# The bias of the damage units as three bf16 rows in TensorE's strain product, and gelus without a bias pointer

## The chip, the core and the metric

The kernel runs on one core of a Trainium2 chip. Its metric is the device time of one execution in microseconds, as the median of several runs. A core has a matrix engine (TensorE, PE in the rows), a vector engine (VectorE, DVE), an activation engine (ScalarE, ACT), a general engine (GpSimd, POOL) and a queue engine for transfers (SyncE, SP). They run side by side and wait for each other through semaphores. Each executes its own instructions in order.

## What is computed

Two layers act on x of 4 x 512 x 128. Each adds an attention and a mixture of experts. The change touches the first layer's attention alone, for 16 heads with 16 units each, a window of 64 steps:

```python
disp_win = _windows(disp, delta)
strain = disp_win - disp[:, :, :, None, :]
bond_act = gelu(strain @ W_strain + rel_emb @ W_pos)
bond_logits = (bond_act @ W_bond)[..., 0]
damage_act = gelu(strain @ W_dmg + b_dmg)
damage = sigmoid((damage_act @ W_dmg_out)[..., 0] + b_dmg_out[0])
logits = bond_logits - 10.0 * damage
```

The product with W_dmg is linear, so the kernel multiplies first and takes the difference of the windows afterwards: the damage units at offset j need gelu(AD[t + j] - AD[t + 63] + b_dmg). b_dmg has 16 values, one for each unit, and the same ones for each head.

## The kernel before

**Setup** (0 to 41 us). x is normalised, turned and multiplied into `AD` (128 partitions = 8 heads x 16 units; index 0 holds the bond units, 1 the damage units; 4 batches of 576 columns, of which 512 are time steps). ScalarE's queue issues small loads at its start, the last nine of them on `d_attn_w`; ScalarE, VectorE and TensorE each wait for all nine. VectorE builds `eyes` near the end of its list (L359 to L361: an identity and a negative identity of 32 x 32, bf16, in three blocks of partitions), then adds the residual (L365), takes the gates' scores from TensorE (L367) and makes the routing (L140 to L169). Within this it waits once for an exp of ScalarE (L429), which stands in ScalarE's list behind the copies of `AD` and two of the turned weights.

**The bank phases** (41 to 327.6 us and 406 to 693 us), one for each of two groups of eight heads. Each has 64 items, one for each offset j, in eight rounds of eight. An item has a bond half and a damage half, each of 128 partitions x 4 batches x (T - t0) columns; t0 is 60 at the first items and falls to 0. VectorE's `strain` (L580) makes the bond half in a ring of four slots; in most items of n not in `PE_ITEMS` (1, 2, 4, 6, 7) it makes the damage half as well, with `bdmg` as its scalar. For items in `PE_ITEMS` TensorE makes the damage half into two PSUM banks (`SD`), half an item at a time (L747): the fp32 values of AD are split into three bf16 parts that stand one below the other in `DS` (partitions 0 to 31, 32 to 63, 64 to 95), and a product with the identity over 96 partitions adds the parts up again. Eight matmuls bring in column t + j with the identity, eight subtract column t + 63 with the negative one. ScalarE takes the gelu of such a half from PSUM and adds the bias through a pointer (L672 and L677, `bias=bdmg[:, 0:1]`), and between them the gelu of the bond half (L675). For the other items one gelu takes both halves from the ring (L667). TensorE reduces every item to logits (L725), and its count `items_reduced` frees the slot for VectorE. Between the items VectorE, ScalarE and TensorE work on the experts: `hidden` (L754) needs w1s, a copy made by POOL (L567), `glu_in` (L600) takes its result, `expert_out` (L760) and `combine` (L612) end it.

**The head of a phase.** ScalarE and VectorE make the three parts; SP carries them to `DS` (L554, 12 transfers, `d_parts`) once POOL has cleared the pads of DS (L558, L559; `ds_zero`). POOL then copies w1s (`stage(0)`), and fills parts of Z. VectorE makes the items 0 to 2, waits for `d_parts` and takes the first hidden product (`glu_in(0)`). TensorE starts with `hidden(0)`, and waits for `d_parts` before its first strain.

**The tail.** After the last item of VectorE what is left runs in a chain through ScalarE's gelus of the items 5 to 7, TensorE's strains and reductions, the last expert's output, the tanh (L682) and VectorE's L595.

Of the kernel before, what the change touches and what calls it, by code (L numbers as in the profile page):

```python
# [11 lines left out]
F32 = mybir.dt.float32  # L12
# [8 lines left out]
P = 128  # L21
# [73 lines left out]
def dram_rows(tensor, offset, dims):  # L95
    return bass.AP(tensor=tensor.tensor, offset=tensor.offset + offset, ap=dims)
# [75 lines left out]
def first_layer(nc, t_in, l0, sb, psum, sem, ident, ACC, nhalf, stats, mv, rstd, carried):  # L172
# [14 lines left out]
    bdo = sb("bdo", [P, 1], F32, l0)  # L187
    wval = sb("wval", [P, C], F32, l0)
    lones = sb("lones", [P, 4, 32], F32, l0)
    eyes = sb("eyes", [P, 2, 32], BF16, l0)  # L190
    AD = sb("AD", [P, 2, B, TP], F32, l0)
    Z = sb("Z", [P, JQ, T], F32, l0)

# [9 lines left out]
    with ExitStack() as su:  # L203
# [16 lines left out]
        gscT = sb("gscT", [P, T], F32, su)  # L220
        gb = sb("gb", [P, E0], F32, su)
        scl = sb("scl", [P, 1], F32, su)
        mask8 = sb("mask8", [P, HG], F32, su)
        ones8 = sb("ones8", [P, HG], F32, su)
        mt = sb("mt", [WIN, WIN], F32, su)
# [86 lines left out]
        def _(v):  # L312
# [30 lines left out]
            scaled(0, 1, TF, tf_ready)  # L343
            scaled(1, 1, TF, tf_ready)
            scaled(3, 0, XN, xn_ready)
            v.wait_ge(d_attn_w, 16 * 9)
            v.wait_ge(const_ready, 2)
            for s in range(2):
                v.tensor_tensor(wblk[:, s, :, :], wrep[:, s, :].unsqueeze(1).to_broadcast([P, HG, BD]),
# [7 lines left out]
                for a in range(4):  # L357
                    last = v.tensor_scalar(lred[:, s, a, a:32:4], mask8[:], wcol[:, s:s + 1], None, ALU.mult)
            for n in range(3):  # L359
                v.tensor_copy(eyes[32 * n:32 * n + 32, 0, :], ident[32 * n:32 * n + 32, 32 * n:32 * n + 32])  # L360
                v.tensor_scalar(eyes[32 * n:32 * n + 32, 1, :], ident[32 * n:32 * n + 32, 32 * n:32 * n + 32], -1.0, None, ALU.mult)  # L361
            v.tensor_scalar(bdo[:], bdo[:], 0.5, None, ALU.mult)

            v.wait_ge(xn_ready, B)
# [8 lines left out]
        def _(act):  # L373
            wd = t_in["L0_attn_W_disp"]
            with nc.allow_non_contiguous_dma(reason="small weights"):
                act.dma_start(gw[:], t_in["L0_ffn_gate_w"]).then_inc(d_gate_w, 16)
                act.dma_start(rel[:], t_in["L0_attn_rel_pos_emb"]).then_inc(d_gate_w, 16)
                act.dma_start(b1r[:], t_in["L0_ffn_mlp1_b"]).then_inc(d_gate_w, 16)
                act.dma_start(wdisp[:], wd.rearrange("k (g n) -> k g n", g=G)).then_inc(d_gate_w, 16)
                for s, n in enumerate(("L0_attn_W_strain", "L0_attn_W_dmg")):  # L380
                    act.dma_start(wrep[:, s, :], dram_rows(t_in[n], 0, [[0, HG], [BD, BD], [1, BD]])).then_inc(d_attn_w, 16)
                act.dma_start(wpos[:], dram_rows(t_in["L0_attn_W_pos"], 0, [[BD, BD], [0, HG], [1, BD]])).then_inc(d_attn_w, 16)
                act.dma_start(scl[:], dram_rows(t_in["L0_ffn_scale"], 0, [[1, P], [1, 1]])).then_inc(d_attn_w, 16)
                for s, n in enumerate(("L0_attn_W_bond", "L0_attn_W_dmg_out")):
                    act.dma_start(wcol[:, s:s + 1], dram_rows(t_in[n], 0, [[0, HG], [1, BD], [1, 1]])).then_inc(d_attn_w, 16)
                act.dma_start(gb[:], dram_rows(t_in["L0_ffn_gate_b"], 0, [[0, P], [1, E0]])).then_inc(d_attn_w, 16)
                act.dma_start(bdmg[:], dram_rows(t_in["L0_attn_b_dmg"], 0, [[0, HG], [1, BD], [1, 1]])).then_inc(d_attn_w, 16)
                act.dma_start(bdo[:], dram_rows(t_in["L0_attn_b_dmg_out"], 0, [[0, P], [1, 1]])).then_inc(d_attn_w, 16)

            def turned_rows(b):  # L390
# [15 lines left out]
            turned_rows(0)  # L406
            turned_rows(1)
            turned_rows(2)
            act.wait_ge(d_attn_w, 16 * 9)
            turned_gates(0)  # L410
            turned_gates(1)
            turned_weights(0)
# [24 lines left out]
        def _(pe):  # L437
# [36 lines left out]
            weights(0)  # L474
            weights(1)
            pe.wait_ge(misc_sb, 1)
            pe.wait_ge(d_attn_w, 16 * 9)
            pe.matmul(S[0][:, 256:256 + WIN], wpos[:].rearrange("k h c -> k (h c)"), relT[:], start=True, stop=True).then_inc(misc_pe, 1)
            rows(3)
            pe.wait_ge(blk_ready, 2)  # L480
# [48 lines left out]
    for g in range(G):  # L529
        with ExitStack() as lp:  # L530
# [16 lines left out]

            @block.sync
            def _(sp):
                sp.wait_ge(ds_zero, g + 1)  # L550
                for n, ready in enumerate((part1, part2, part3)):
                    sp.wait_ge(ready, g + 1)
                    for q in range(4):
# [3 lines left out]
            def _(pool):  # L557
                pool.memset(DS[0:96, :, :, 0:PAD], 0.0)  # L558
                pool.memset(DS[0:96, :, :, PAD + T:TP], 0.0).then_inc(ds_zero, 1)  # L559
                if g == 0:  # L560

                    pool.sem_inc(items_reduced, RING)  # L562
# [97 lines left out]
            def _(act):  # L660
                def gelu(n, it, between=None):
# [7 lines left out]
                    f = 2 * pe_item(g, it, n)  # L669
                    tiles = ring[:, slot, 0, :, t0:T]  # L670
                    act.wait_ge(sd_ready, f + 1)
                    act.activation(ring[:, slot, 1, 0:2, t0:T], SD[:, :, t0:T], ACT.Gelu, bias=bdmg[:, 0:1]).then_inc(sd_taken, 1)  # L672
                    if between:
                        between()
                    act.activation(tiles, tiles, ACT.Gelu)  # L675
                    act.wait_ge(sd_ready, f + 2)
                    act.activation(ring[:, slot, 1, 2:4, t0:T], SD[:, :, t0:T], ACT.Gelu, bias=bdmg[:, 0:1]).then_inc(gelu_done, 1)  # L677

                def tanh(par, q):
                    act.wait_ge(items_reduced, RING + N0 + 4 * q + 4)  # L680
# [36 lines left out]
            def _(pe):  # L717
# [11 lines left out]
                def strain(n, it, half):  # L729
# [10 lines left out]
                    elif it:  # L740
                        pe.wait_ge(gelu_done, N0 + 8 * it - 8 + PE_ITEMS[-1] + 1)
                    if n == FIRST_PE_ITEMS[0] and it == 0 and half == 0:
                        pe.wait_ge(d_parts, 192 * (g + 1))
                    for sign, at in ((0, j + t0), (1, PAD + t0)):
                        for i in range(2):
                            for q in range(4):
                                mm = pe.matmul(SD[32 * q:32 * q + 32, i, t0:T], eyes[0:96, sign, :], DS[0:96, q, 2 * half + i, at:at + T - t0],  # L747
                                               start=(sign == 0), stop=(sign == 1))
                    mm.then_inc(sd_ready, 1)

                def hidden(c, u, staged):
# [1344 lines left out]
```

## Time and profile before

| | us |
|---|---|
| median of three runs | 1254.11 |
| lowest and highest run | 1249.81, 1258.18 |
| span of the profiled execution | 1203.6 |
| TensorE busy | 1056.1 (88%) |
| VectorE busy | 962.4 (80%) |
| ScalarE busy | 821.7 (68%) |
| POOL busy | 168.1 (14%) |

The span goes from the first to the last instruction of one execution; the time of a run also holds what lies around it. Busy time of TensorE is modelled, since its matmuls are pipelined. The shares are means over phases of different kinds, so the phases are to be read one by one.

### The profile page before, as it was taken

How to read it: one execution, taken by the hardware profiler on the slowest of the kernel's cores; microseconds unless marked ns; L12 is line 12 of the kernel's file. 1: busy time of each engine (PE TensorE's matmuls, PEld its weight loads, DVE VectorE, ACT ScalarE, POOL GpSimd, SP SyncE). 2: the span in 40 equal slices, each digit the busy share in tenths (PEclk: the TensorE clock that was granted, in tenths of full speed). 3: DMA queues.
4: the chain of work that ended last, by engine and by line, in shares of the span. 5: the costliest groups of instructions: out<-in, count | busy, mean ns of one | idle time of the engine just before them, and what ended most of it. 6: DMA issues, size and time to landing. Idle time of an engine off the chain costs nothing. (4 is left out here: it accounts for less than half of the span.)

```text
span 1203.6 us, 23755 instructions
## 1 busy us (share of the span) xinstructions
PE 1056.1 (88%) x9995; PEld 567.0 (47%) x9995; DVE 962.4 (80%) x1193; ACT 821.7 (68%) x888; POOL 168.1 (14%) x265
## 2 busy tenths in 40 slices
PE   6499888998879499889899868999999999999897
PEld 4233333333368333333333368853654565655533
DVE  7899999999763799999999863557778577676757
ACT  3689999999763489999989862243156666665464
POOL 5100000000140100000000050232760000000072
PEclk9699999999979789999999979999779999999899
DMA  8400000000075200000000057000132344523121
GB/s 269 128 2 2 1 1 2 1 1 2 1 204 145 54 1 2 1 1 2 1 1 2 1 172 178 24 1 1 36 105 62 105 132 125 155 80 90 47 60 45
DMA packets 71754, 67.45 MB, mean 56 GB/s; under 512 B 6148, under 2 KB 63200, under 8 KB 71648
## 3 DMA queue, kind: packets, MB, share of 16 engines
q1 hardware_dynamic: 66264, 55.31, 16.1%
q0 software_dynamic: 3840, 10.43, 3.3%
q8 instruction: 79, 1.29, 0.4%
q10 hardware_dynamic: 1544, 0.20, 0.1%
q14 instruction: 27, 0.22, 0.1%
HBM read 41.80 MB, written 20.97 MB: 52 GB/s over the span
## 5 line engine op out<-in xcount | busy, mean ns | idle before, releaser
L580 DVE SCALAR_TENSOR_TENSOR ring<-AD,PT 128x1808 f32<-128x1808 f32 (+15 forms) x128 | 286.1, 2235 | 3.8 <-POOLq L562 1.9
L725 PE MATMUL LG<-ring,lred 128*32 128x456 f32 (+15 forms) x2048 | 233.4, 575 | 2.0 <-ACT ring L677 2.0
L1932 DVE TENSOR_REDUCE MX<-SS 128x2 f32<-128x1024 f32 x119 | 144.6, 1219 | 55.3 <-PE SS L1649 55.2
L1862 ACT ACTIVATE EX<-SS 128x1024 f32<-128x1024 f32 x128 | 130.4, 1031 | 80.4 <-PE SS L1649 79.8
L667 ACT ACTIVATE ring<-ring 128x3616 f32<-128x3616 f32 (+15 forms) x50 | 169.9, 3398 | 3.7 <-DVE ring L580 3.7
L747 PE MATMUL SD<-DS,eyes 96*32 96x456 bf16 (+15 forms) x2496 | 156.2, 369 | 10.1 <-ACT ring L672 8.1
L675 ACT ACTIVATE ring<-ring 128x1824 f32<-128x1824 f32 (+15 forms) x78 | 141.0, 1808 | 0.0
L747 PEld LDWEIGHTS SD<-DS,eyes 96*32 96x32 bf16 x2496 | 58.0, 96 | 154.6 <-ACT ring L672 56.7
L580 DVE SCALAR_TENSOR_TENSOR ring<-AD,bdmg 128x1808 f32<-128x1808 f32 (+15 forms) x50 | 111.4, 2228 | 0.0
L725 PEld LDWEIGHTS LG<-ring,lred 128*32 128x32 f32 x2048 | 59.4, 110 | 100.2 <-issue 76.6
L760 PE MATMUL PY<-w2T,xg 128*128 128x128 f32 x512 | 75.6, 292 | 31.5 <-DVE xg L605 31.5
L754 PE MATMUL PH<-tT,w1s 128*128 128x512 f32 x128 | 74.5, 666 | 30.2 <-DVE xg L600 23.2
L672 ACT ACTIVATE ring<-SD,bdmg 128x912 f32<-128x912 f32 (+15 forms) x78 | 82.8, 1062 | 23.6 <-PE SD L747 21.7
L760 PEld LDWEIGHTS PY<-w2T,xg 128*128 128x128 f32 x512 | 63.2, 194 | 66.0 <-DVE xg L605 51.5
L677 ACT ACTIVATE ring<-SD,bdmg 128x912 f32<-128x912 f32 (+15 forms) x78 | 82.6, 1059 | 2.4 <-PE SD L747 1.5
L612 DVE SCALAR_TENSOR_TENSOR ACC<-PY,route,ACC 128x128 f32<-128x128 f32 x256 | 72.7, 359 | 9.2 <-PE PY L760 9.2
L567 POOL COPY w1s<-w1T 128x128 f32<-128x128 f32 x16 | 11.6, 724 | 463.9 <-PE PH L754 463.9
L1649 PE MATMUL SS<-KS,QS 32*128 32x512 f32 x238 | 62.1, 515 | 14.2 <-DVE MX L1932 12.3
L1839 ACT ACTIVATE HB<-PHh,b1c 128x128 f32<-128x128 f32 x156 | 44.6, 371 | 38.1 <-PE PHh L1601 37.8
L1669 PE MATMUL PW<-EX,VA 128*32 128x512 f32 x512 | 68.5, 609 | 0.0
L1649 PE MATMUL SS<-QS,KS 32*128 32x512 f32 x256 | 65.1, 509 | 3.2 <-ACT EX L1862 2.1
L1984 DVE RECIPROCAL attT<-attT 128x128 f32<-128x128 f32 (+1 forms) x58 | 54.5, 959 | 0.2
(346 smaller groups left out, 1558.0 us busy)
## 6 DMA issues: line engine op xcount, KB each, us to landing
w1s<-in_L_ffn_W SPq DMA_DIRECT2D x39, 256.0 KB, 3.0
w2s<-in_L_ffn_W SPq DMA_DIRECT2D x39, 256.0 KB, 2.9
band<-zs SPq DMA_DIRECT2D x8, 1024.0 KB, 9.9
wide<-band POOLq DMA_DIRECT2D x16, 380.0 KB, 8.3
wide<-band SPq DMA_DIRECT2D x16, 380.0 KB, 10.0
band<-Z SPq DMA_DIRECT2D x4, 1024.0 KB, 7.7
xs<-Z SPq DMA_DIRECT2D x4, 640.0 KB, 8.0
xl<-xs SPq DMA_DIRECT2D x10, 256.0 KB, 2.9
```

What stands on the lines that cost most here:

```text
L580: return v.scalar_tensor_tensor(out=ring[:, slot, s, :, t0:T], in0=AD[:, s, :, j + t0:j + T], scalar=extra, in1=AD[:, s, :, PAD + t0:PAD + T],
L667: act.activation(tiles, tiles, ACT.Gelu).then_inc(gelu_done, 1)
L672: act.activation(ring[:, slot, 1, 0:2, t0:T], SD[:, :, t0:T], ACT.Gelu, bias=bdmg[:, 0:1]).then_inc(sd_taken, 1)
L675: act.activation(tiles, tiles, ACT.Gelu)
L677: act.activation(ring[:, slot, 1, 2:4, t0:T], SD[:, :, t0:T], ACT.Gelu, bias=bdmg[:, 0:1]).then_inc(gelu_done, 1)
L725: mm = pe.matmul(LG[32 * b:32 * b + 32, par, s, t0:T], lred[:, s, n % 4, :], ring[:, slot, s, b, t0:T], start=(n % 4 == 0), stop=(n % 4 == 3))
L747: mm = pe.matmul(SD[32 * q:32 * q + 32, i, t0:T], eyes[0:96, sign, :], DS[0:96, q, 2 * half + i, at:at + T - t0], start=(sign == 0), stop= ...
L754: pe.matmul(PH[:], w1s[:], tT[:, c, :], start=True, stop=True).then_inc(h_ready, 1)
L760: mm = pe.matmul(PY[:, i, :], xg[:, c % 2, P * i:P * i + P], w2T[:, bass.ds(HG * g + it, 1), :].rearrange("p o c -> p (o c)"), start=True, ...
L1649: mm = pe.matmul(bank[:, n, :], rows[r:r + 32, b % 2, q, P * t:P * t + P], cols[r:r + 32, b % 2, q, :], start=True, stop=True)
L1862: act.activation(EX[:, Q % 2, hh:hh + 2, t, :], SS[:, slot, :, :], ACT.Exp, scale=SCALE1).then_inc(freed[slot], 1)
L1932: v.tensor_reduce(MX[:, t, p // 2, hh:hh + 2], pairs_of(b, name), AX.X, ALU.max).then_inc(freed[slot], 1)
```

## The change

The bias of the damage units goes into the product of the strain. `eyes` has five blocks: four positive ones and a negative one. DS gets three more partitions (96 to 98) that hold 1.0 everywhere, and block q of `eyes` has in these three rows the bf16 parts of the 32 biases of its output rows. The first eight matmuls of a half item now take 99 partitions and block q, the other eight take 96 and the negative block as before. The gelus of L672 and L677 lose their bias argument. The bias is loaded a second time as a row on three partitions (one more transfer in ScalarE's queue, so that three engines wait for ten), and VectorE splits it in seven small operations, each waiting for the one before. POOL sets the ones after the pads and waits for this before it copies w1s; TensorE waits for it before the first strain.

```diff
@@ -187,7 +187,7 @@
     bdo = sb("bdo", [P, 1], F32, l0)
     wval = sb("wval", [P, C], F32, l0)
     lones = sb("lones", [P, 4, 32], F32, l0)
-    eyes = sb("eyes", [P, 2, 32], BF16, l0)
+    eyes = sb("eyes", [P, 5, 32], BF16, l0)
     AD = sb("AD", [P, 2, B, TP], F32, l0)
     Z = sb("Z", [P, JQ, T], F32, l0)
 
@@ -220,6 +220,8 @@
         gscT = sb("gscT", [P, T], F32, su)
         gb = sb("gb", [P, E0], F32, su)
         scl = sb("scl", [P, 1], F32, su)
+        brow = sb("brow", [P, 2, P], F32, su)
+        bpart = sb("bpart", [P, 4, P], BF16, su)
         mask8 = sb("mask8", [P, HG], F32, su)
         ones8 = sb("ones8", [P, HG], F32, su)
         mt = sb("mt", [WIN, WIN], F32, su)
@@ -343,7 +345,7 @@
             scaled(0, 1, TF, tf_ready)
             scaled(1, 1, TF, tf_ready)
             scaled(3, 0, XN, xn_ready)
-            v.wait_ge(d_attn_w, 16 * 9)
+            v.wait_ge(d_attn_w, 16 * 10)
             v.wait_ge(const_ready, 2)
             for s in range(2):
                 v.tensor_tensor(wblk[:, s, :, :], wrep[:, s, :].unsqueeze(1).to_broadcast([P, HG, BD]),
@@ -357,8 +359,19 @@
                 for a in range(4):
                     last = v.tensor_scalar(lred[:, s, a, a:32:4], mask8[:], wcol[:, s:s + 1], None, ALU.mult)
             for n in range(3):
-                v.tensor_copy(eyes[32 * n:32 * n + 32, 0, :], ident[32 * n:32 * n + 32, 32 * n:32 * n + 32])
-                v.tensor_scalar(eyes[32 * n:32 * n + 32, 1, :], ident[32 * n:32 * n + 32, 32 * n:32 * n + 32], -1.0, None, ALU.mult)
+                v.tensor_copy(eyes[32 * n:32 * n + 32, 0:4, :],
+                              ident[32 * n:32 * n + 32, 32 * n:32 * n + 32].unsqueeze(1).to_broadcast([32, 4, 32]))
+                v.tensor_scalar(eyes[32 * n:32 * n + 32, 4, :], ident[32 * n:32 * n + 32, 32 * n:32 * n + 32], -1.0, None, ALU.mult)
+            r = slice(96, 99)
+            link(v.tensor_copy(bpart[r, 0, :], brow[r, 0, :]))
+            link(v.tensor_tensor(brow[r, 1, :], brow[r, 0, :], bpart[r, 0, :], ALU.subtract))
+            link(v.tensor_copy(bpart[r, 1, :], brow[r, 1, :]))
+            link(v.tensor_tensor(brow[r, 0, :], brow[r, 1, :], bpart[r, 1, :], ALU.subtract))
+            link(v.tensor_scalar(bpart[r, 3, :], bpart[r, 0, :], ident[r, 96:97], 1.0, ALU.mult, ALU.mult))
+            link(v.scalar_tensor_tensor(out=bpart[r, 2, :], in0=bpart[r, 1, :], scalar=ident[r, 97:98], in1=bpart[r, 3, :],
+                                        op0=ALU.mult, op1=ALU.add))
+            v.scalar_tensor_tensor(out=eyes[r, 0:4, :].rearrange("p q m -> p (q m)"), in0=brow[r, 0, :], scalar=ident[r, 98:99],
+                                   in1=bpart[r, 2, :], op0=ALU.mult, op1=ALU.add)
             v.tensor_scalar(bdo[:], bdo[:], 0.5, None, ALU.mult)
 
             v.wait_ge(xn_ready, B)
@@ -385,6 +398,7 @@
                     act.dma_start(wcol[:, s:s + 1], dram_rows(t_in[n], 0, [[0, HG], [1, BD], [1, 1]])).then_inc(d_attn_w, 16)
                 act.dma_start(gb[:], dram_rows(t_in["L0_ffn_gate_b"], 0, [[0, P], [1, E0]])).then_inc(d_attn_w, 16)
                 act.dma_start(bdmg[:], dram_rows(t_in["L0_attn_b_dmg"], 0, [[0, HG], [1, BD], [1, 1]])).then_inc(d_attn_w, 16)
+                act.dma_start(brow[96:99, 0, :], dram_rows(t_in["L0_attn_b_dmg"], 0, [[0, 3], [0, HG], [1, BD]])).then_inc(d_attn_w, 16)
                 act.dma_start(bdo[:], dram_rows(t_in["L0_attn_b_dmg_out"], 0, [[0, P], [1, 1]])).then_inc(d_attn_w, 16)
 
             def turned_rows(b):
@@ -406,7 +420,7 @@
             turned_rows(0)
             turned_rows(1)
             turned_rows(2)
-            act.wait_ge(d_attn_w, 16 * 9)
+            act.wait_ge(d_attn_w, 16 * 10)
             turned_gates(0)
             turned_gates(1)
             turned_weights(0)
@@ -474,7 +488,7 @@
             weights(0)
             weights(1)
             pe.wait_ge(misc_sb, 1)
-            pe.wait_ge(d_attn_w, 16 * 9)
+            pe.wait_ge(d_attn_w, 16 * 10)
             pe.matmul(S[0][:, 256:256 + WIN], wpos[:].rearrange("k h c -> k (h c)"), relT[:], start=True, stop=True).then_inc(misc_pe, 1)
             rows(3)
             pe.wait_ge(blk_ready, 2)
@@ -547,7 +561,7 @@
 
             @block.sync
             def _(sp):
-                sp.wait_ge(ds_zero, g + 1)
+                sp.wait_ge(ds_zero, 2 * g + 1)
                 for n, ready in enumerate((part1, part2, part3)):
                     sp.wait_ge(ready, g + 1)
                     for q in range(4):
@@ -557,6 +571,8 @@
             def _(pool):
                 pool.memset(DS[0:96, :, :, 0:PAD], 0.0)
                 pool.memset(DS[0:96, :, :, PAD + T:TP], 0.0).then_inc(ds_zero, 1)
+                pool.memset(DS[96:99], 1.0).then_inc(ds_zero, 1)
+                pool.wait_ge(ds_zero, 2 * g + 2)
                 if g == 0:
 
                     pool.sem_inc(items_reduced, RING)
@@ -669,12 +685,12 @@
                     f = 2 * pe_item(g, it, n)
                     tiles = ring[:, slot, 0, :, t0:T]
                     act.wait_ge(sd_ready, f + 1)
-                    act.activation(ring[:, slot, 1, 0:2, t0:T], SD[:, :, t0:T], ACT.Gelu, bias=bdmg[:, 0:1]).then_inc(sd_taken, 1)
+                    act.activation(ring[:, slot, 1, 0:2, t0:T], SD[:, :, t0:T], ACT.Gelu).then_inc(sd_taken, 1)
                     if between:
                         between()
                     act.activation(tiles, tiles, ACT.Gelu)
                     act.wait_ge(sd_ready, f + 2)
-                    act.activation(ring[:, slot, 1, 2:4, t0:T], SD[:, :, t0:T], ACT.Gelu, bias=bdmg[:, 0:1]).then_inc(gelu_done, 1)
+                    act.activation(ring[:, slot, 1, 2:4, t0:T], SD[:, :, t0:T], ACT.Gelu).then_inc(gelu_done, 1)
 
                 def tanh(par, q):
                     act.wait_ge(items_reduced, RING + N0 + 4 * q + 4)
@@ -740,12 +756,16 @@
                     elif it:
                         pe.wait_ge(gelu_done, N0 + 8 * it - 8 + PE_ITEMS[-1] + 1)
                     if n == FIRST_PE_ITEMS[0] and it == 0 and half == 0:
+                        pe.wait_ge(ds_zero, 2 * g + 2)
                         pe.wait_ge(d_parts, 192 * (g + 1))
-                    for sign, at in ((0, j + t0), (1, PAD + t0)):
-                        for i in range(2):
-                            for q in range(4):
-                                mm = pe.matmul(SD[32 * q:32 * q + 32, i, t0:T], eyes[0:96, sign, :], DS[0:96, q, 2 * half + i, at:at + T - t0],
-                                               start=(sign == 0), stop=(sign == 1))
+                    for i in range(2):
+                        for q in range(4):
+                            pe.matmul(SD[32 * q:32 * q + 32, i, t0:T], eyes[0:99, q, :], DS[0:99, q, 2 * half + i, j + t0:j + T],
+                                      start=True, stop=False)
+                    for i in range(2):
+                        for q in range(4):
+                            mm = pe.matmul(SD[32 * q:32 * q + 32, i, t0:T], eyes[0:96, 4, :], DS[0:96, q, 2 * half + i, PAD + t0:PAD + T],
+                                           start=False, stop=True)
                     mm.then_inc(sd_ready, 1)
 
                 def hidden(c, u, staged):
```

## Rows read from the trace of the kernel before

**Rows 1.** Busy times by stretch, us: stretch, length, PE, PEld, DVE, ACT, POOL, clock, DMA.

```profile
100.00:300.00 200.00, 182.88 (x1936) 72.75 (x1928) 200.00 (x217) 188.10 (x144) 4.09 (x6) 0.99 0.01 1
300.00:327.60 27.60, 23.08 (x228) 9.29 (x228) 21.50 (x31) 22.21 (x17) 0.00 (x0) 1.00 0.00 1
```

**Rows 2.** What VectorE waited for, 41 to 327.6 us: total us, times, longest.

```profile
DVE ACC L612 <- PE PY L760: 4.6, 3, 2.9
DVE Z L595 <- ACT Z L682: 2.6, 2, 1.5
DVE ring L580 <- PE LG L725: 0.8, 1, 0.8
DVE xg L600 <- DMA DS<-xg: 0.4, 1, 0.4
```

**Rows 3.** The page's costliest groups: busy us, mean ns, idle before: the bank gelus.

```profile
L672 ACT ACTIVATE ring<-SD,bdmg 128x912 f32<-128x912 f32 (+15 forms) x78 | 82.8, 1062 | 23.6 <-PE SD L747 21.7
L677 ACT ACTIVATE ring<-SD,bdmg 128x912 f32<-128x912 f32 (+15 forms) x78 | 82.6, 1059 | 2.4 <-PE SD L747 1.5
```

**Rows 4.** Groups of one shape (60 to 320 us), and the page's exp from PSUM.

```profile
L672 ACT ACTIVATE ring<-SD,bdmg 128x1024 f32<-128x1024 f32 x3 | 3.3, 1108 | 0.1
L1862 ACT ACTIVATE EX<-SS 128x1024 f32<-128x1024 f32 x128 | 130.4, 1031 | 80.4 <-PE SS L1649 79.8
```

**Rows 5.** Instructions in order of time, tail of the first phase: start us, us.

```profile
313.94 1.09 ACT L672 ACTIVATE ring<-SD,bdmg 128x1024 f32<-128x1024 f32 x1
...
319.05 1.11 ACT L672 ACTIVATE ring<-SD,bdmg 128x1024 f32<-128x1024 f32 x1
...
320.22 1.05 PE L747 MATMUL SD<-DS,eyes 96*32 96x512 bf16 x16 [0.19 <-ACT ring L672]
...
321.09 1.89 PE L725 MATMUL LG<-ring,lred 128*32 128x512 f32 x16
...
324.11 1.13 DVE L612 SCALAR_TENSOR_TENSOR ACC<-PY,route,ACC 128x128 f32<-128x128 f32 x4 [2.92 <-PE PY L760]
```

**Rows 6.** POOL's memset of 4096 elements by shape; the copy of w1s, min/median/max ns.

```profile
L1476 POOL MEMSET VA<- 128x4096 f32 x1 | 3.5, 3511 | 3.9 <-POOLq L1107 3.9
L567 POOL COPY w1s<-w1T x16: 289/729/1474, 42.0 to 645.0; 128x128 f32<-128x128 f32 x16
```

**Rows 7.** Instructions in order of time, head of the first phase.

```profile
41.10 0.94 POOL L558 MEMSET DS<- 96x1008 bf16 x1 [16.47 <-POOLq L203]
...
41.16 2.10 DVE L580 SCALAR_TENSOR_TENSOR ring<-AD,PT 128x1808 f32<-128x1808 f32 x1 [1.88 <-POOLq L562]
...
42.03 1.39 POOL L567 COPY w1s<-w1T 128x128 f32<-128x128 f32 x1
...
43.47 2.07 PE L754 MATMUL PH<-tT,w1s 128*128 128x512 f32 x2 [3.05 <-POOL w1s L567]
...
49.74 2.10 DVE L580 SCALAR_TENSOR_TENSOR ring<-AD,PT 128x1808 f32<-128x1808 f32 x1
...
56.27 0.75 DVE L600 TENSOR_SCALAR xg<-PH,b1T 128x512 f32<-128x512 f32 x1 [0.41 <-DMA DS<-xg]
```

**Rows 8.** Instructions in order of time, setup.

```profile
8.22 0.61 ACTq L387 DMA_DIRECT2D bdmg<-in_L_attn_b_dmg  x1
...
8.87 2.31 ACTq L388 DMA_DIRECT2D bdo<-in_L_attn_b_dmg_out  x1
...
18.64 1.26 ACT L402 ACTIVATE tT<-su,scl 128x512 f32<-128x512 f32 x2 [1.72 <-DMA bdo<-in_L_attn_b_dmg_out]
...
28.38 0.42 DVE L367 TENSOR_TENSOR gsc<-su,gb 128x256 f32<-128x256 f32 x1 [1.17 <-PE su L499]
...
32.99 0.29 DVE L156 TENSOR_TENSOR c<-c 128x128 f32<-128x128 f32 x1
...
37.21 0.41 ACT L429 ACTIVATE route<-route 128x256 f32<-128x256 f32 x1
...
37.65 0.42 DVE L166 TENSOR_TENSOR route<-route,gt 128x256 f32<-128x256 f32 x1 [2.33 <-ACT route L429]
```

## The prediction

> **What bounds the kernel now.** The span of the profiled execution is 1203.6 us, the median of the runs 1254.11 us, so 50.5 us lie around the span; I take them as fixed and make the sum against the median. The change works in two bank phases (41 to 327.6 us, and again from 406 us), so I read the busy times of each engine by stretch first. From 100 to 300 us VectorE is busy for 200.00 of 200 us, ScalarE for 188.1, TensorE for 182.9 [rows 1]; the second phase reads the same. The reader is to see that ScalarE has 11.9 us and TensorE 17.1 us free there, and VectorE none. The end of the phase is different: from 300 to 327.6 us VectorE is busy for 21.50 and ScalarE for 22.21 of 27.6 us, so there other engines set the pace.
>
> Next the waits of VectorE over the whole phase: 4.6 us for TensorE's PY in 3 waits, 2.6 us for ScalarE's tanh in 2, 0.8 us for the first reduction, 0.4 us for the DMA of the strain parts [rows 2]. That is 8.4 us of 286, and none of it lies between 100 and 300 us. What ScalarE or TensorE save in between frees nothing: VectorE's item (L580) is what the next gelu waits for.
>
> **The gelus without a pointer.** 156 bank gelus (L672 and L677, 78 each) take 82.8 and 82.6 us together [rows 3]. Each has its input in PSUM and its bias in `bdmg`. At 1024 columns one takes 1108 ns; the nearest activation without a pointer, the exp of the second layer, also from PSUM and of 1024 columns, has a mean of 1031 ns [rows 4]. I take 77 ns a gelu. The other end is nothing (were the new form to read a constant by pointer all the same). 156 x 0.077 = 12.0 us of ScalarE's busy time, 6.0 us a phase. The Trainium skill, ScalarE: Activation LUTs (What ACT_TABLE_LOAD costs), states about 93 ns for each pointer operand; by that it would be 14.5 us. Either way it is busy time of an engine that is not the bound.
>
> How much of it reaches the end? At the tail I follow the order in time [rows 5]. The chain runs through L672 of item 6, its other tiles, L677 of item 6, then TensorE's strain for item 7, L672 of item 7 at 319.05, TensorE's second strain at 320.22, reduction at 321.09, an expert's product, and VectorE's L612 at 324.11 after a wait of 2.92 us. Three bank gelus lie in this chain (L672 and L677 of item 6, L672 of item 7); L677 of item 7 runs beside the reduction. So the tail shrinks by 3 x 0.077 = 0.23 us. At the head, VectorE's one wait for PY stands behind the strain that waits for one L672: 0.08 us. With 0.31 us a phase, both give 0.6 us. The lower bound is 0. The upper one is all of the 8.0 us that other engines cost VectorE [rows 2], which needs a gain ten times that of the gelus in the chains, so it is no end of the range.
>
> **TensorE's strain with 99 rows.** The number of matmuls stays: 16 for each half item, the same columns, the same accumulation; only the first eight take 99 rows for 96 and another slice of `eyes`. 16 of them with 512 columns take 1.05 us, 16 passes of the fp32 reduction with 128 rows and 512 columns 1.89 us [rows 5]. Those are the ends: nothing, and the price of the row with 128 rows (another type, hence far off). I take nothing, since three rows in 96 even at a cost in proportion to rows would be 0.03 us a group, 78 groups a phase, 2.6 us, which lies in TensorE's free time: 17.1 of 200 us [rows 1], about 22 us over the 260 us of the phase with strains, or 0.29 us a group. Without that cover it would be 5 us in all.
>
> **The row of ones by POOL.** The memset of DS[96:99] is 4 x 4 x 576 = 9216 bf16 elements in each partition. The memset of 1008 such elements took 0.94 us [rows 7], one of 4096 fp32 elements 3.51 us [rows 6]: 0.83 ns an element. So 0.94 + 8208 x 0.00083 = 7.8 us. It stands ahead of the copy of w1s (L567), ended until now at 43.4 us, and of the fill of Z, which nobody waits for. POOL is free for the copy at 42.0 + 7.8 = 49.8 us. The copy takes 1.39 us there and ends with VectorE's item that began before it [rows 7]; over all copies it takes 289 to 1474 ns [rows 6]. The item beginning at 49.74 ends at 51.8, so I put the copy's end at 52.0. The first expert product (2.07 us there) then ends at 54.1. VectorE takes it at 56.27, and waited there for a DMA, not for the product [rows 7]. Margin 2.1 us: cost nothing. SP's DMAs wait for the pads' memset alone (the count stays the first of the two), so d_parts comes as before; TensorE's new wait for the ones stands before its first strain, and that comes later than the 56.27 us of L600. If the cover were gone, each us of POOL beyond a 9.9 us memset would delay VectorE by one, twice.
> The Trainium skill, SBUF — State Buffer (Who interferes with whom), says that the port pair which VectorE and GpSimd share is an exclusive lock for whoever comes first, and excepts GpSimd instructions that only write; without that exception the memset would hold VectorE's items, at the price of the rival below. The rows bear the exception out: the item at 41.16 took 2.10 us beside the memset of 0.94, and the one at 49.74, with POOL idle, 2.10 as well [rows 7].
>
> **The setup.** ScalarE's queue issues one DMA more, ahead of `bdo`'s. The nearest issues took 0.61 us (`bdmg`) and 2.31 us (`bdo`, which came into a backlog) [rows 8]; I take 0.6. ScalarE itself, VectorE and TensorE wait for the last of these at 18.64 us, 7.5 us after its issue, when the large weights are in; so it comes 0 to 2.3 us later, I take 0.6. Behind ScalarE's wait stand the turned gates, behind VectorE's the block weights, the lower tiles and its new work. That work: three copies wider by 96 columns, 0.1 us each, and seven operations of 128 columns on three partitions, each waiting for the one before. One of 128 columns took 0.29 us [rows 8]; 0.32 with the wait, so 2.2 us; 2.5 us in all. VectorE had idle time behind it: 1.17 us before L367, and 2.33 us at L166 while ScalarE came late to its exp (0.41 us of it is the exp): 1.9 us of slack [rows 8]. 0.6 + 2.5 = 3.1 us against 1.17 + 1.9 = 3.1 us. So it just fits: I take 0.1 us; the upper end is 2.3 + 2.5 - 3.1 = 1.7 us. What is late next, once the slack is gone, is ScalarE's exp, behind it two turned weights, TensorE's mask transposes and the barrier.
>
> **The sum.** 1254.1 - 0.6 (gelus in the chains) + 0.1 (setup) + 0 (strain, POOL) = 1253.6 us.
>
> **Rivals.**
> *The saved time of ScalarE reaches the end* (faster). It would if the items were paced by ScalarE: 12 us off, 1242. For it: ScalarE is busy for 94% of the stretch. Against: VectorE has no gap in 200 us [rows 1], and its waits name ScalarE for 2.6 us only [rows 2]. Chance 0.06.
> *The setup is late*: the extra DMA lands 2.3 us later. 1254.1 - 0.6 + 1.7 = 1255.2. For it: the 2.31 us issue beside it. Against: it lands long after its issue anyway. Chance 0.11.
> *The gelus are no shorter*: 1254.2. Against: the other gelus of the kernel name no second input in their rows. Chance 0.03.
> *POOL's memset is in VectorE's way* (slower): in the first 8 us of each phase, either holding VectorE off its items or running at half speed. If it holds VectorE for its length, 2 x 7.8 = 15.6 us: 1269. It decides once the memset is longer than 9.9 us or an item beside it takes more than 2.10; over 1% from 6.3 us a phase. Against: the row at 41.16. Chance 0.04.
> *TensorE becomes the bound* (slower): if a strain group costs over 0.29 us more. At 4/3 of its time (the fourth group of 32 rows counted as a full one): 0.33 x 78 - 22 = 3.7 us a phase, 1261; at the reduction's price, 0.84 x 78 - 22 = 43.5 a phase, 1341. For it: the extra rows open the last 32. Against: the reduction runs with 128 rows beside it without trouble. Chance 0.02.
>
> **How the numbers follow.** The forecast has 0.74. A measurement of this kernel tells about 1% from no change (its three runs lie from 1249.8 to 1258.2). Faster by over 1% is the first rival, 0.06; slower by over 1% are the last two, 0.06; the rest, 0.88, is within 1%. The range: the forecast's own uncertainty is -0.6 to 0 for the gelus and 0 to 1.7 for the setup, 1253.5 to 1255.8; the runs themselves spread by about 4 us to either side. 1249 to 1259 holds the forecast, the late setup and the useless pointer; left out are the rivals with 0.06 and 0.06.
>
> **What would show it.** Gelus of L672 and L677 near 1030 ns at 1024 columns: the saving is real; VectorE still 200.00 of 200 us and ScalarE down by 4 us in the same stretch: it isn't on the path. POOL's memset of 7.8 us ending near 50, the first PH product ending near 54, VectorE's L600 still near 56.3 and still behind the DMA. The waits before L367 and L166 gone, the phase beginning at 41.1 to 41.3. TensorE's groups of 16 at 1.05 us. Wrong would be: a first L600 that waits for PH, items longer than 2.10 us beside the memset, a phase beginning past 42, or gaps of VectorE between 100 and 300 us.

## The result, and the profile after

| | before | after |
|---|---|---|
| median of six runs each, us | 1258.09 | 1271.88 |
| span of the profiled execution, us | 1203.6 (see below) | 1268.2 |
| ratio after to before | | 1.0118, 95% interval 1.0097 to 1.0140 |

The changed kernel is slower by 1.2%, 12 to 18 us. The forecast was no change.

The trace of before and the runs of before don't belong together: profiled again (c0), the kernel before has a span of 1257.5 us for 1203.6, and all of the 54 us lie in the second layer, behind the skew stage of the second phase (481.3 against 425.9 us). So the 50.5 us that the prediction put "around the span" were not there; in the run profiled after the change the time is 1.8 us more than the span. Kernels were timed in batches, each with the kernel before beside them, and the batches have two levels, whatever the kernel: the medians of the kernel before are 1256.1, 1205.6, 1204.3 and 1254.5 us in the four batches of the experiments. In the second layer the granted clock is 0.88 in c0 and 0.95 in the trace of before, and every trace of the longer level has waits for a source that the profile can only call remote, where none of the shorter level has one. The largest of them in c0 (total us, times, longest):

```profile
ACT EX L1862 <- remote: 59.2, 10, 26.9
```

What this source is, and what sets the level, stays open. The batches of 1204.3 and 1254.5 us carry the same chip number, so a fixed difference between chips isn't shown. Every ratio below is taken within one batch, against the kernel before. That a cost is the same at both levels isn't shown.

First what VectorE waited for in the changed kernel, from 41 to 360 us (total us, times, longest). It answers [rows 2].

```profile
DVE ring L596 <- POOLq L578: 10.7, 1, 10.7
DVE ACC L628 <- PE PY L780: 4.5, 3, 2.8
DVE Z L611 <- ACT Z L698: 2.5, 2, 1.5
...
DVE xg L616 <- DMA DS<-xg: 0.4, 1, 0.4
```

The others are near those of before. The first is new in its size: one wait of 10.7 us of VectorE's item for POOL's queue at line 578. Line 578 is `pool.sem_inc(items_reduced, RING)`. In order of time, the head of the first phase after the change; it answers [rows 7]:

```profile
38.84 1.90 ACT L723 CAST ring<-AD 128x2048 bf16<-128x2048 f32 x1 [0.29 <-PEq L203]
39.91 7.77 POOL L574 MEMSET DS<- 3x9216 bf16 x1
...
47.77 2.10 DVE L596 SCALAR_TENSOR_TENSOR ring<-AD,PT 128x1808 f32<-128x1808 f32 x1 [10.71 <-POOLq L578]
48.08 1.93 POOL L583 COPY w1s<-w1T 128x128 f32<-128x128 f32 x1 [0.40 <-POOL DS L574]
...
52.20 1.90 ACT L725 CAST ring<-ring 128x2048 bf16<-128x2048 f32 x1 [11.46 <-DVE ring L663]
...
62.86 0.75 DVE L616 TENSOR_SCALAR xg<-PH,b1T 128x512 f32<-128x512 f32 x1 [0.40 <-DMA DS<-xg]
```

The reader is to see that VectorE begins 0.09 us after POOL's memset of ones ends (39.91 + 7.77 = 47.68), that ScalarE, which depends on VectorE's remainder of the split, stands still with it (11.46 us, for 2.58 in c0), and that L616 still waits for the DMA at its end: everything behind the first item is shifted as a whole. The phase takes 295.3 us, from the memset of the pads to L893, against 286.6.

The head of the second phase has the same memset and no such wait, for the increments are made in the first phase only:

```profile
414.25 0.94 POOL L572 MEMSET DS<- 96x1008 bf16 x1 [35.08 <-POOLq L825]
...
414.29 2.10 DVE L596 SCALAR_TENSOR_TENSOR ring<-AD,PT 128x1808 f32<-128x1808 f32 x1 [0.32 <-PEq L825]
...
415.35 7.77 POOL L574 MEMSET DS<- 3x9216 bf16 x1
...
423.18 1.83 POOL L583 COPY w1s<-w1T 128x128 f32<-128x128 f32 x1
...
425.06 2.07 PE L774 MATMUL PH<-tT,w1s 128*128 128x512 f32 x2 [12.31 <-POOL w1s L583]
...
429.31 0.75 DVE L616 TENSOR_SCALAR xg<-PH,b1T 128x512 f32<-128x512 f32 x1 [0.39 <-DMA DS<-xg]
```

This phase takes 286.9 us. Here the expert's product ends at 427.1, 2.2 us before VectorE takes it.

The page's groups after the change (busy us, mean ns | idle before), for [rows 3]:

```profile
L763 PE MATMUL SD<-DS,eyes 99*32 99x456 bf16 (+15 forms) x1248 | 92.6, 373 | 5.5 <-ACT ring L688 4.0
...
L688 ACT ACTIVATE ring<-SD 128x912 f32<-128x912 f32 (+15 forms) x78 | 75.8, 972 | 30.0 <-PE SD L767 27.0
L767 PE MATMUL SD<-DS,eyes 96*32 96x456 bf16 (+15 forms) x1248 | 91.7, 369 | 0.0
...
L693 ACT ACTIVATE ring<-SD 128x912 f32<-128x912 f32 (+15 forms) x78 | 75.7, 970 | 4.4 <-PE SD L767 3.8
```

A bank gelu takes 972 ns for 1062: 90 ns less, 13.9 us over 156. The idle time before those of L688 rises by 6.4 us (23.6 to 30.0), and the busy times of the stretch show why nothing came of it, for [rows 1]:

```profile
100.00:300.00 200.00, 184.04 (x1932) 75.32 (x1928) 200.00 (x217) 183.08 (x142) 3.61 (x6) 0.98 0.01 1
```

ScalarE is busy for 183.1 us instead of 188.1, VectorE for 200.00 as before.

### The profile page after: what moved, and what is told of

Its sections match the earlier page's. It is cut to its first block and busy times, and to the rows that moved or that the text cites. A ratio compares the mean times of both kernels' runs of the same rounds, so it can differ in the third digit from the quotient of the medians.

```text
span 1268.2 us, 23767 instructions
## 1 busy us (share of the span) xinstructions
PE 1074.8 (85%) x9995; PEld 576.8 (45%) x9995; DVE 964.2 (76%) x1200; ACT 809.7 (64%) x888; POOL 184.0 (15%) x267
## 5 line engine op out<-in xcount | busy, mean ns | idle before, releaser
L596 DVE SCALAR_TENSOR_TENSOR ring<-AD,PT 128x1808 f32<-128x1808 f32 (+15 forms) x128 | 283.4, 2214 | 11.9 <-POOLq L578 10.7
L780 PE MATMUL PY<-w2T,xg 128*128 128x128 f32 x512 | 75.6, 292 | 37.5 <-DVE xg L621 37.0
L763 PE MATMUL SD<-DS,eyes 99*32 99x456 bf16 (+15 forms) x1248 | 92.6, 373 | 5.5 <-ACT ring L688 4.0
L688 ACT ACTIVATE ring<-SD 128x912 f32<-128x912 f32 (+15 forms) x78 | 75.8, 972 | 30.0 <-PE SD L767 27.0
L767 PE MATMUL SD<-DS,eyes 96*32 96x456 bf16 (+15 forms) x1248 | 91.7, 369 | 0.0
L1669 PE MATMUL SS<-QS,KS 32*128 32x512 f32 x256 | 68.8, 537 | 26.5 <-ACT EX L1882 21.5
L693 ACT ACTIVATE ring<-SD 128x912 f32<-128x912 f32 (+15 forms) x78 | 75.7, 970 | 4.4 <-PE SD L767 3.8
L763 PEld LDWEIGHTS SD<-DS,eyes 99*32 99x32 bf16 x1248 | 25.3, 95 | 116.9 <-ACT ring L688 48.6
L1689 PE MATMUL PW<-EX,VA 128*32 128x512 f32 x512 | 73.5, 650 | 0.0
## 6 DMA issues: line engine op xcount, KB each, us to landing
band<-zs SPq DMA_DIRECT2D x8, 1024.0 KB, 11.2
```

What stands on the lines that cost most here:

```text
L596: return v.scalar_tensor_tensor(out=ring[:, slot, s, :, t0:T], in0=AD[:, s, :, j + t0:j + T], scalar=extra, in1=AD[:, s, :, PAD + t0:PAD + T],
L763: pe.matmul(SD[32 * q:32 * q + 32, i, t0:T], eyes[0:99, q, :], DS[0:99, q, 2 * half + i, j + t0:j + T], start=True, stop=False)
L767: mm = pe.matmul(SD[32 * q:32 * q + 32, i, t0:T], eyes[0:96, 4, :], DS[0:96, q, 2 * half + i, PAD + t0:PAD + T], start=False, stop=True)
L780: mm = pe.matmul(PY[:, i, :], xg[:, c % 2, P * i:P * i + P], w2T[:, bass.ds(HG * g + it, 1), :].rearrange("p o c -> p (o c)"), start=True, ...
L1669: mm = pe.matmul(bank[:, n, :], rows[r:r + 32, b % 2, q, P * t:P * t + P], cols[r:r + 32, b % 2, q, :], start=True, stop=True)
L1689: mm = pe.matmul(PN[32 * hh:32 * hh + 32, :], VA[:, b % 2, t, 4 * q + hh, :], EX[:, q % 2, hh, t, :], start=(t == 0), stop=(t == NT - 1))
```

## The experiments

The stages in every trace, in us. A bank phase runs from POOL's memset of the pads (L558 in the kernel before) to VectorE's addition of the mask (L873), a skew stage from there to the next phase, or to the norm of the second layer (L1150). The column band<-zs is the median time from the issue of this DMA to its landing. Each length comes from a single profiled execution.

| kernel | phase 1 | skew 1 | phase 2 | skew 2 | band<-zs | ratio to before (95%) |
|---|---|---|---|---|---|---|
| before | 286.6 | 78.5 | 286.7 | 84.8 | 9.9 | |
| after | 295.3 | 80.1 | 286.9 | 87.4 | 11.2 | 1.0118 (1.0097 to 1.0140) |
| c0 before again | 286.5 | 79.2 | 287.1 | 85.4 | 9.9 | 1.0003 (0.9979 to 1.0026) |
| e1 increments first | 286.5 | 81.0 | 286.0 | 85.8 | 10.9 | 1.0035 (1.0017 to 1.0054) |
| e2 ones alone | 295.8 | 79.7 | 286.8 | 85.7 | 9.9 | 1.0085 (1.0052 to 1.0118) |
| e3 no pointer | 287.0 | 79.0 | 286.6 | 85.4 | 9.7 | 1.0006 (0.9983 to 1.0029) |
| e4 setup alone | 287.1 | 80.5 | 286.6 | 86.6 | 11.2 | 1.0036 (1.0013 to 1.0058) |
| e5 mended | 286.9 | 80.2 | 286.1 | 86.3 | 11.3 | 1.0031 (1.0006 to 1.0056) |
| e6 six items, before | 300.1 | 77.5 | 299.0 | 85.5 | 9.6 | 1.0235 (1.0191 to 1.0278) |
| e7 six items, mended | 295.1 | 79.9 | 294.7 | 86.3 | 11.0 | 1.0169 (1.0125 to 1.0213) |
| e8 +192 bytes | 286.9 | 80.8 | 286.8 | 87.5 | 11.3 | 1.0027 (1.0011 to 1.0043) |
| e9 mended, padded | 286.9 | 79.0 | 286.4 | 86.2 | 10.3 | 1.0013 (0.9985 to 1.0040) |
| e10, e13 +128 bytes | 286.8, 286.7 | 79.3, 78.8 | 286.4, 286.6 | 84.9, 86.5 | 11.0, 10.8 | e13: 0.9989 (0.9969 to 1.0009) |
| e11 +64 bytes | 287.0 | 80.4 | 287.0 | 87.3 | 11.2 | one run |
| e12 +256 bytes | 287.1 | 78.8 | 286.8 | 85.4 | 9.7 | 0.9997 (0.9981 to 1.0013) |

**c0, the kernel before.** No edit.

> The kernel before, unchanged, for a profile beside those that follow. The profiled execution that the prediction was read from had a span of 1203.6 us, 50 less than its runs. If that trace was a rare short execution, this one's span is near 1255 us and the extra 50 us lie behind 790 us, in the second layer, as they do in the changed kernel's trace. If instead the time lies around the span, the span is again near 1204.

Its span is 1257.5 us, its median 1257.42. The long second layer comes with the batch, whatever the kernel.

**e1, the increments first.** The changed kernel with this order on POOL:

```diff
 def _(pool):
+    if g == 0:
+        pool.sem_inc(items_reduced, RING)
+        ...
     pool.memset(DS[0:96, :, :, 0:PAD], 0.0)
     pool.memset(DS[0:96, :, :, PAD + T:TP], 0.0).then_inc(ds_zero, 1)
     pool.memset(DS[96:99], 1.0).then_inc(ds_zero, 1)
     pool.wait_ge(ds_zero, 2 * g + 2)
-    if g == 0:
-        pool.sem_inc(items_reduced, RING)
-        ...
```

> The changed kernel with POOL's four semaphore increments put ahead of its memsets, nothing else. Theory A (the increments stood behind the memset of ones, and VectorE's first item waits for them): the first item starts at once, the first bank phase falls from 295.3 to 286.6 us, the time by 8.7 us against the changed kernel, to about 1263. Theory B (the memset is in the way for its writes, or another edit costs the time): at most 1 us less, about 1271.

The first phase is back at 286.5 us, and the ratio falls from 1.0118 to 1.0035. In its trace VectorE begins with the phase, beside the same memset:

```profile
39.46 2.10 DVE L596 SCALAR_TENSOR_TENSOR ring<-AD,PT 128x1808 f32<-128x1808 f32 x1 [1.86 <-PEq L203]
39.73 0.94 POOL L578 MEMSET DS<- 96x1008 bf16 x1 [15.93 <-POOLq L203]
40.61 0.17 POOL L579 MEMSET DS<- 96x16 bf16 x1
40.83 7.78 POOL L580 MEMSET DS<- 3x9216 bf16 x1
...
43.68 2.10 DVE L596 SCALAR_TENSOR_TENSOR ring<-AD,bdmg 128x1808 f32<-128x1808 f32 x1
```

The item at 43.68 runs wholly beside the memset in its 2.10 us. Theory A holds, and the memset is in nobody's way as a memset. What remains, 0.35% (0.17 to 0.54), needs another cause.

**e2, the ones alone.** The kernel before with two lines more on POOL (and SP's count adapted):

```diff
     pool.memset(DS[0:96, :, :, PAD + T:TP], 0.0).then_inc(ds_zero, 1)
+    pool.memset(DS[96:99], 1.0).then_inc(ds_zero, 1)
+    pool.wait_ge(ds_zero, 2 * g + 2)
```

> The kernel before with only POOL's memset of DS[96:99] and its wait added, where the change put them; nothing reads the ones. Theory A: the first bank phase takes 295 us, the time rises by 8.7 us, ratio 1.007. Theory B (the cost comes from the split of the bias, the extra DMA, or the gelus): ratio 1.000.

First phase 295.8 us, ratio 1.0085; VectorE's first item waits 10.8 us for POOL's queue. The cost comes with these two lines alone.

Which of the two? The edit takes them together, but the other traces tell. In every kernel without the added wait in front of the increments, VectorE's first item begins 0.06 to 0.07 us after the pads' memset *begins*, though the increments stand behind that memset in POOL's program: 41.10 and 41.16 in [rows 7], 37.96 and 38.02 in c0. In e5 below, where the ones and their wait come later, it is the same:

```profile
39.60 0.94 POOL L576 MEMSET DS<- 96x1008 bf16 x1 [15.69 <-POOLq L205]
...
39.66 2.10 DVE L601 SCALAR_TENSOR_TENSOR ring<-AD,PT 128x1808 f32<-128x1808 f32 x1 [2.25 <-POOLq L580]
```

So the 0.94 us memset doesn't hold the increments back; the line that does is `pool.wait_ge(ds_zero, 2 * g + 2)`, which sends them off only when all three memsets are done. Whether the increments would also pass a memset of 7.77 us, with the wait put behind them, was not tried.

**e3, no pointer.** `bias=bdmg[:, 0:1]` taken out of L672 and L677 and nothing put in its place; the kernel leaves b_dmg out of the bank items.

> The kernel before with the bias argument of the bank gelus (L672, L677) left out and nothing in its place, so the bank items leave b_dmg out. Theory A: ScalarE's busy time falls by about 13.9 us (156 gelus, 89 ns each as in the changed kernel's trace) and the time by 0.6 us, ratio 0.999 to 1.000. The rival, that shorter gelus shift the second layer or the loops for the worse and carry the part of the loss that the memset leaves open (5 us): ratio 1.004.

Ratio 1.0006, the phases as before. The gelus' 13.9 us bring nothing that can be measured, and cost nothing; the interval is too wide (0.17% less to 0.29% more) to tell the predicted 0.6 us from none.

**e4, the setup alone.**

```diff
-    eyes = sb("eyes", [P, 2, 32], BF16, l0)
+    eyes = sb("eyes", [P, 5, 32], BF16, l0)
+    act.dma_start(brow[96:99, 0, :], ...).then_inc(d_attn_w, 16)
-    v.wait_ge(d_attn_w, 16 * 9)
+    v.wait_ge(d_attn_w, 16 * 10)
+    link(v.tensor_copy(bpart[r, 0, :], brow[r, 0, :]))
+    ...
```

> The kernel before with only the setup's edits: the bias loaded as a row (one DMA more, three engines wait for ten), eyes of five blocks, the seven linked operations. No memset, no 99th row, gelus with their pointer. Theory: VectorE reaches the end of its gate scores about 1.4 us after ScalarE is free for the exp, the setup ends 1.4 us later, ratio 1.001, and the bank phases take 286.6 us as before. Rival (this part carries what the first experiment left over, 3.5 to 4.4 us, by the layout of SBUF or the DMAs): ratio 1.0035.

1.0036 (1.0013 to 1.0058): more than the theory's 1.001, and what the rival said. Its trace has two differences. VectorE is late for the exp:

```profile
34.73 0.42 ACT L443 ACTIVATE route<-route 128x256 f32<-128x256 f32 x1 [1.36 <-DVE route L164]
```

And band<-zs lands in 11.2 us for 9.9, with both skew stages longer, long after the setup is over. All kernels profiled so far with the larger `eyes` show this, and none of the others does. That formed theory C: the place of the tiles.

**e5, mended.** The whole change, with POOL's increments and w1s copy ahead of the ones, and the seven operations moved into VectorE's wait for the exp:

```diff
     stage(0)
+    pool.wait_ge(w1_staged, HG * g + 1)
+    pool.memset(DS[96:99], 1.0).then_inc(ds_zero, 1)
+    pool.wait_ge(ds_zero, 2 * g + 2)
 ...
 v.tensor_tensor(route[:], scores[:], ..., ALU.subtract).then_inc(exp_ready, 1)
+if between:
+    between()
 v.wait_ge(exp_done, 1)
```

> The changed kernel with all its work, moved: POOL's increments first, then the copy of w1s, then the memset of ones; and VectorE's seven operations into its wait for the exp. Theory: POOL's part costs nothing, the split about 0.2 us, the gelus give 0.6 us back, so ratio 0.9995 to 1.001 against the kernel before. Rival (the 99th row, the extra DMA or the shifted layout cost 3 to 4 us by themselves): ratio 1.003.

Ratio 1.0031, what the rival said. The first phase is at 286.9 us, so the queue's cost is gone; the skew stages keep theirs.

**e6 and e7, six bank items of eight.** `PE_ITEMS` and `FIRST_PE_ITEMS` get item 3; TensorE's `strain(3, it, 0)` and `strain(3, it, 1)` go around `reduce(2)`, and item 4's behind them; `hidden(2)` and `reduce(3)` each move by a place. e6 is this on the kernel before, e7 on the mended one.

> The kernel before with item 3 of every eight given to TensorE as well (six bank items for five), pointers kept. VectorE loses 8 items of 2.24 us a phase (17.9 us), TensorE gains 8 x 1.96 = 15.7 us, ScalarE 8 x (1.8 + 2 x 1.06 - 3.41) = 4.1 us of 258. If VectorE's busy time is what paces the phase, as the prediction held, the phases get shorter until ScalarE paces them: about 278 us each, ratio 0.987. If TensorE or the order of waits paces it: 1.000 or above.

> The mended kernel with the same sixth bank item. Once ScalarE paces the phase, its shorter gelus count: 94 gelus a phase x 0.09 = 8.4 us. So if theory holds for both, this is 8 to 16 us faster than the sixth item with pointers, ratio about 0.975. If the gelus' saving is worth nothing here either, it equals that one.

Both are slower than the kernel before, where both were expected faster. Busy times from 100 to 300 us, e6 and then e7:

```profile
100.00:300.00 200.00, 182.47 (x2035) 74.01 (x2026) 181.70 (x203) 182.72 (x148) 1.76 (x6) 1.00 0.01 1
```

```profile
100.00:300.00 200.00, 186.09 (x2072) 75.52 (x2068) 185.33 (x208) 180.57 (x151) 1.78 (x6) 1.00 0.01 1
```

VectorE is busy for 182 of 200 us, and so are the two others: no engine is full, and the phase is 13 us longer all the same. The waits point to ScalarE and TensorE, which wait for each other over the two banks: in these 200 us the gelus of L672 wait 16.4 us for TensorE's strains in e6, and 4.2 in c0. No run shows by itself that this paces the phase. Here the shorter gelus may count: e7's phases are 5.0 and 4.3 us shorter than e6's, of 8.4 expected. But e7 has the whole mended change, the two kernels had four runs each, and their intervals overlap. Whether another order of the strains makes six items pay was not tried.

**e8 to e13, nothing but bytes.** The kernel before with tiles declared after `eyes` moved in SBUF by spare bytes in each partition; e9 is the mended kernel with 64 spare bytes, 256 in all.

```diff
-    eyes = sb("eyes", [P, 2, 32], BF16, l0)
+    eyes = sb("eyes", [P, 5, 32], BF16, l0)          # e8
+    spare = sb("spare", [P, 64], BF16, l0)           # e10, e13: 128 bytes; e11 [P, 32]: 64; e12 [P, 128]: 256
```

> The kernel before with nothing but eyes declared with five blocks, as the change declares it: every tile declared later lies 192 bytes further in each partition. Theory C (the rest of the loss is the layout: in all four traces with the larger eyes band<-zs lands in 10.9 to 11.3 us instead of 9.6 to 9.9, xs<-Z in 9.2 to 9.8 instead of 8.0 to 8.8, and the two stages after the bank phases are 2.6 us longer together): ratio 1.002, band<-zs about 11.1. Rival (the longer landings come with the extra DMA or the 99th row): ratio 1.000, band<-zs 9.8.

> The mended kernel with 64 bytes left free behind eyes, so that the later tiles lie 256 bytes further than before instead of 192. Theory C with the grain at 128 or 256 bytes: band<-zs back at 9.8 us, the two stages 2.6 us shorter, ratio 1.001 against the kernel before. If the layout isn't the cause, as the mended one: 1.003.

> The kernel before with 128 bytes left free behind eyes. Theory C: if the grain is 128 bytes, band<-zs 9.8 us; if it is 256, about 11.

> The kernel before with 64 bytes left free behind eyes. Theory C, whichever grain: band<-zs about 11 us, xs<-Z above 9. If only the amount of 192 bytes mattered: 9.8.

> The kernel before with 256 bytes left free behind eyes, nothing else. If the later tiles' place to a grain of 256 bytes sets the cost: band<-zs near 9.8 us and ratio 1.000. If any move costs: ratio 1.002 to 1.003, band<-zs 10.3 or more.

> The kernel before with 128 bytes left free behind eyes, now timed. If the long landings (11.0 us for band<-zs) carry the cost: ratio 1.002 to 1.003. If they don't, as the stages' lengths of 79.3 and 84.9 us in the single look say: 1.000.

DMA issues (count, KB each, median us to landing), e8 and then e12:

```profile
band<-zs SPq DMA_DIRECT2D x8, 1024.0 KB, 11.3
...
xs<-Z SPq DMA_DIRECT2D x4, 640.0 KB, 9.6
```

```profile
band<-zs SPq DMA_DIRECT2D x8, 1024.0 KB, 9.7
...
xs<-Z SPq DMA_DIRECT2D x4, 640.0 KB, 8.5
```

A shift of 192 bytes alone costs 0.27% (0.11 to 0.43), 3.2 us. A shift of 256 costs nothing that can be measured and has the short landings; 64, 128 and 192 have the long ones. Yet 128 bytes cost nothing either, in 12 runs. So the long landing is not by itself the price: of the two outcomes written down for e13 the second came. One gap is left in this: e8 was timed at the short level, e12 and e13 at the long one, and no shift alone was timed at both (e10's single run, at the short level, is 1206.3 us for a median of 1204.3). The first skew stage goes another way: at most 79.7 us for shifts of 0, 128 and 256, at least 79.9 for 64 and 192. The gap between the groups is small beside the 77.5 to 79.7 us of the unshifted kernels, so a grain of 128 bytes is a guess, and what would wait on it stays open. The padded mended kernel measures 1.0013, its interval includes both none and the mended kernel's 1.0031, its skew stages together are 1.3 us shorter for the 2.6 expected, and its landing of 10.3 us lies between the two groups. So padding is not shown to mend the change.

No kernel was found that beats the kernel before.

## Why the prediction was wrong

**The step that failed** is in the part on POOL: the memset "stands ahead of the copy of w1s (L567) ... and of the fill of Z". It named these two as all that is queued behind it. The diff shows a third thing between them: four increments of semaphores, no instruction that a busy time would show, and VectorE's first item waits for the first of them. [rows 7] had it in the line of the item at 41.16, "[1.88 <-POOLq L562]": released by POOL's queue at line 562. I used this line for its 2.10 us and did not read its releaser. The margin of 2.1 us that I worked out for the copy was right (2.2 in the second phase), but it belonged to the later of two things behind the memset. The second half of the same step is the wait: the prediction counted the memset's length and gave no price to the `wait_ge` behind it. Before the change the increments passed the pads' memset (0.06 us from its begin to VectorE's first item); now they wait from 38.82 to 47.77, 8.95 us. The difference, 8.9 us, is the two pads' memsets up to 39.91 (1.09), the memset of ones (7.77) and 0.09, less the 0.06. By the lengths of the phases the cost is 8.8 us; e2 against c0 and the changed kernel's first phase against its second give 9.3 and 8.4.
Of the signs that the prediction named, one would have told: "VectorE's L600 still near 56.3". It came at 62.86, 24.0 us into its phase for 15.2.
The rival that ended slower had the right place (POOL's memset, the first 8 us) and the wrong mechanism: it priced the memset at both phases, for holding VectorE off its items. e1 shows that it doesn't, and only the first phase pays.

**The setup.** Predicted 0.1 us. The terms were right (VectorE's new work 2.3 us for 2.5), the slack was not. Of the two waits I added up, the 1.17 us ahead of L367 [rows 8] belonged to that execution, where the last of the small loads landed at 18.64 us, in c0 at 16.84; in c0 L367 begins without a wait, and 1.8 us in front of L166 is all there is. ScalarE waited 1.38 us for VectorE before the exp in the changed kernel, 1.36 in e4. The ratios of e4 and e8 differ by 0.09%, 1.1 us, which fits but is within their intervals. The begin of the first phase can't tell: it lies between 37.5 and 41.1 us in the traces whose setup is that of before, and at 38.8 in the changed kernel.

**What was not in the prediction**: the place of the tiles behind `eyes`, 3.2 us by e8 (1.3 to 5.2). That the place costs is measured; by what mechanism isn't known.

**The sum** by the runs: 8.8 (queue) + 3.2 (place) + 1.1 (setup) + 0 (gelus) = 13.1 us. Measured 1.18% of 1258 = 14.8 us, 12.2 to 17.6. It closes within the interval; the term of the queue is shown by e1, e2 and the traces, the term of the place has its own wide interval, and that of the setup is not distinct from nothing.

**The gelus.** Predicted 77 ns each and 0.6 us in the end; measured 90 ns, and nothing that shows (e3). The Trainium skill, ScalarE: Activation LUTs (What ACT_TABLE_LOAD costs), with its 93 ns for a pointer operand, was nearer than the row of the exp that I took. That VectorE paces the stretch and ScalarE's time is not on the path held: 200.00 of 200 us, ScalarE down by 5.0.

**The strain with 99 rows.** Predicted nothing. The mean is 373 ns for a matmul with 99 rows and 369 for one with 96, the mean of before, and the second phase is as long as before.

**POOL's memset** was predicted at 7.8 us from two rows and took 7.77.

**The absolute time.** The forecast of 1253.6 was made against a median of three runs, 1254.11, and a span from the other level. With six runs the median of before is 1258.09; the range of 1249 to 1259 would have been 4 us too low at its centre even for no change.

## What to carry to other kernels

Before work is put into an engine's queue, list everything behind it in program order, with the semaphore increments and waits that have no duration, and for each who waits for it; the releasers in the trace ("<-POOLq L562") name them. Look at an added wait first: here increments passed a memset ahead of them, and were held by a wait for it. An initial credit that others start on belongs ahead of every wait of its queue. A slack read from one execution, where a DMA happened to be late, is no slack: look for it in a second trace. And a declaration that only grows a tile can cost: here 192 bytes cost 3.2 us, so time a change of layout alone.

## What the runs showed of the hardware

With no wait between a memset of 0.94 us and POOL's semaphore increments behind it, VectorE's item that waits for these began 0.06 us after the memset had begun (the same within 0.01 us in all thirteen such traces); with a wait for the memsets between them it began 8.95 us after the first of them.

POOL's memsets took time by their free size, on few partitions as on many: 9216 bf16 elements in 7.77 us on 3 partitions, 1008 in 0.94 us on 96. Beside the memset of 7.77 us VectorE's items with two SBUF inputs kept their 2.10 us (e1).

A shift of all later tiles by 64, 128 or 192 bytes went with a longer landing of a 1 MB store from SBUF: 10.8 to 11.3 us, for 9.6 to 9.9 without a shift. By 256 bytes it was 9.7 us in the kernel before and 10.3 in the mended one. The Trainium skill, DMA: Bandwidth & Descriptors (How a descriptor splits into AXI transactions), says that a transaction must start from an address at a multiple of 256 bytes, and that a descriptor which starts elsewhere also fetches the bytes from the multiple below it and pays for them. The landings of the kernels that were only shifted agree with that grain, though no trace gives the address of zs; the time of the kernel (128 bytes cost nothing, 192 cost 0.27%) isn't explained by it.

The second layer of the same kernel took 425.9 us in one execution (granted clock 0.95) and 481.3 in another (0.88, with 59.2 us of waits of one ScalarE line for a remote source), while the bank phases agree to 0.5 us.
